# A transformer layer on 8 cores: the softmax-like normalisation moves to GpSimd, the masks to VectorE, the first layer norm's scaling to ScalarE

## The reference

```python
p = softplus(scores); p = p * p; p = p * causal
attn = p / (sum(p, -1) + 1e-9)
x = layernorm(x + (attn @ v) @ w_proj.T + b_proj)
h = gelu(x @ q8(W_fc).T + b_fc + 2 * (x @ A_fc.T) @ B_fc.T)          # f = 4096
x = layernorm(x + h @ q8(W_proj).T + b_proj + 2 * (h @ A_proj.T) @ B_proj.T)
```

## Time and profile before

| | us |
|---|---|
| median of 3 runs | 2142.27 (2140.19 to 2320.73) |
| the profiled execution | 2140.47 |
| span of its slowest core, core 3 | 2138.9 |
| spans of its cores | 2126.6 to 2138.9 |
| PE busy | 1929.6 (90%), 8834 matmuls |
| DVE busy | 1042.4 (49%) |
| ACT busy | 855.0 (40%) |
| POOL busy | 448.2 (21%) |

### The profile page before, as it was taken

How to read it: one execution, slowest core, us unless ns; L and a number is a source line. 1 busy time by engine, 2 the same in 40 slices (tenths; PEclk the granted TensorE clock), 3 DMA queues, 4 the chain that set the end, 5 groups by cost and what they waited for, 6 DMA issues and landing times.

```text
span 2138.9 us, 26841 instructions; the slowest of 8 cores (2126.6 to 2138.9 us)
## 1 busy us (share of the span) xinstructions
PE 1929.6 (90%) x8834; PEld 759.0 (35%) x8834; DVE 1042.4 (49%) x1613; ACT 855.0 (40%) x1026; POOL 448.2 (21%) x515
## 2 busy tenths in 40 slices
PE   6897987888987899999867889999999999999998
PEld 2332332222322333322222234444444444444443
DVE  2675887766689777788759731111110101020202
ACT  2464765765422466677533421212222121313130
POOL 1121221221156412222225421111010101010201
PEclk9998998999999999999978999999999999999999
DMA  8656554357466443344485465020202111110101
GB/s 130 149 135 146 155 150 131 100 128 149 122 188 181 131 112 116 114 124 128 125 222 163 133 191 169 30 69 30 70 30 59 40 50 50 50 60 20 60 10 49
DMA packets 118023, 228.35 MB, mean 107 GB/s; under 512 B 59282, under 2 KB 59538, under 8 KB 115186
## 3 DMA queue, kind: packets, MB, share of 16 engines
q1 hardware_dynamic: 109042, 195.03, 30.2%
q0 software_dynamic: 8848, 31.63, 8.7%
HBM read 182.21 MB, written 58.98 MB: 113 GB/s over the span
## 4 chain that ended last, share of the span: by engine, by line
PE 72%; DVE 10%; DMA 8%; issue 6%; POOL 2%; ACT 2%; SPq 0%; DVEq 0%; POOLq 0%; ACTq 0%
PE ps_s L924 20%; PE ps_a L976 10%; PE ps_f L976 10%; PE ps_a L718 8%; PE ps_f L341 8%; PE ps_s L674 6%; PE ps_f L365 5%; DVE a_ph L700 3%; DMA a_bc<-recscr 3%; PE ps_f L616 3%; DVE a_QO L776 2%; DMA recscr<-g_rec 2%; PE ps_f L497 2%; DMA g_den<-a_nd 1%; ACT a_ph L685 1%
## 5 line engine op out<-in xcount | busy, mean ns | idle before, releaser
L685 ACT ACTIVATE a_ph<-ps_s 128x1024 bf16<-128x1024 f32 (+1 forms) x576 | 560.7, 976 | 506.8 <-PE ps_s L674 505.4
L931 ACT ACTIVATE b_h<-ps_s,g_bfc,g_scl 128x512 bf16<-128x512 f32 x256 | 199.1, 778 | 649.1 <-PE ps_s L924 649.1
L924 PE MATMUL ps_s<-b_xT,b_Wfc 128*128 128x512 bf16 x2048 | 444.0, 379 | 0.0
L718 PE MATMUL ps_a<-a_ph,a_V 128*65 128x512 bf16 (+3 forms) x1280 | 354.0, 366 | 94.4 <-DVE a_ph L700 73.5
L700 DVE TENSOR_TENSOR a_ph<-a_ph 128x1024 bf16<-128x1024 bf16 (+1 forms) x576 | 399.9, 719 | 24.9 <-ACT a_ph L685 12.8
L341 PE MATMUL ps_f<-a_xT,a_wqk 128*128 128x512 bf16 x1024 | 307.5, 396 | 35.5 <-DMA a_xT<-xT 16.9
L692 POOL TENSOR_TENSOR a_ph<-a_ph,g_mask 128x256 bf16<-128x256 bf16 x256 | 196.4, 785 | 498.6 <-ACT a_ph L685 497.7
L981 DVE SCALAR_TENSOR_TENSOR g_x<-ps_a,g_scl,g_x 128x512 f32<-128x512 f32 x32 | 24.0, 751 | 566.1 <-PE ps_a L976 566.1
L924 PEld LDWEIGHTS ps_s<-b_xT,b_Wfc 128*128 128x128 bf16 x2048 | 200.4, 98 | 241.6 <-issue 0.2
L674 PE MATMUL ps_s<-a_QO,a_K 64*128 64x512 bf16 (+3 forms) x1280 | 226.3, 367 | 2.6 <-ACT a_QO L351 2.5
L976 PE MATMUL ps_a<-b_Wp,b_h 128*128 128x512 bf16 x1024 | 224.4, 379 | 0.0
(11 more groups left out here) (47 smaller groups left out, 937.1 us busy)
## 6 DMA issues: line engine op xcount, KB each, us to landing
a_w<-wfc SPq DMA_DIRECT2D x64, 512.0 KB, 5.7
a_w<-wpF SPq DMA_DIRECT2D x64, 512.0 KB, 4.5
a_bc<-recscr SPq DMA_DIRECT2D x64, 256.0 KB, 4.4
g_x<-x SPq DMA_DIRECT2D x32, 512.0 KB, 4.0
x1scr<-g_x SPq DMA_DIRECT2D x32, 512.0 KB, 4.0
g_x<-x1scr SPq DMA_DIRECT2D x32, 512.0 KB, 3.2
out<-g_x SPq DMA_DIRECT2D x32, 512.0 KB, 2.6
a_wqk<-wqk POOLq DMA_DIRECT2D x16, 512.0 KB, 7.4
```

Of the source, the lines that this page charges most:

```text
L685: s_read[sl] = P.op("scalar", lambda E: E.activation(dst, src, AF.Softplus, scale=HS ** -0.5), waits=[tok, ph_av[q]])
L718: tok = P.op("tensor", lambda E, c0=c0, n=n, off=off, x0=x0, hd=hd, fin=fin: E.matmul(ps_a[0:65, hd * 512 + c0: hd * 512 + c0 + n], V4[:, ...
L924: tok = P.op("tensor", lambda E, cc=cc, c0=c0: E.matmul(ps, b_Wfc[:, c0:c0 + 128], b_xT[:, (g % 2) * 4096 + cc * 512:(g % 2) * 4096 + (cc ...
L931: h_tok[(g, f)] = P.op("scalar", lambda E: E.activation(b_h[:, f * 512:(f + 1) * 512], ps, AF.Gelu, bias=g_bfc[:, f:f + 1], scale=g_scl[:, ...
```

## The change

1. **Normalisation on POOL.** Adding 1e-9 and the inverse (now a power -1, against a tile `g_m1` of -1) and both multiplications are POOL instructions. `pool_op` makes each of POOL's compute instructions wait for the one before it.
2. **Second head in the upper partitions.** The second head's A*V matmul takes 128 weight columns of `a_V`, shifted by one element: row 63 of the result is its denominator and rows 64 to 127 are its values. Its copy is 128x512, `a_bc` holds one head in the lower and one in the upper 64 partitions, and has two buffers, so turns are gone. Fetch and broadcast are two DMAs each instead of one. The relay's ticks are 1, 3, 5, 7 and 9.
3. **Masks on DVE**, behind the square and no longer ahead of it.
4. **First layer norm's scaling on ACT** (second layer norm: DVE as before), with one more small POOL instruction for the bias -mean*scale; it is emitted at the end of a projection chain and not in its middle. The load of x two tiles ahead moves from the chain's start to its middle.
5. **Merges behind the scores.** `merge_some` is called once in a tick, right behind `emit_scores`, and emits a merge if the chain in progress has 1 to 6 matmuls behind it. Merges are spread over windows 5 to 7 and 9 to 13 (before: also 14).
6. **Loads.** The first load of weights and x is split into halves and reordered; the absolute maxima use six slots (three of `a_w`, three of `g_x`).

The diff's core:

```diff
+        def pool_op(fn, waits):
+            pool_last[0] = P.op("gpsimd", fn, waits=list(waits) + [pool_last[0]])
+            return pool_last[0]
...
+        def load_first():
...
+            part(0)
+            rows(0)
+            rows(1)
+            part(1)
...
-                    yield 1.0 + merge_some(cc)
+                    yield 1.0
...
+            return k % 6 if k < 64 else k % 3
...
-        def merge_some(cc):
-
-            if cc not in (3, 6):
-                return 0.0
-            mg["seen"] += 1
-            if mg["want"] and mg["took"] * mg["of"] < mg["seen"] * mg["want"]:
+        def merge_some(part):
+
+            if not chains or mg["took"] >= mg["want"] * part:
+                return
+            c = chains[0]
+            if c.key[0] in ("qk", "v") and 1 <= c.done <= 6:
                 mg["took"] += 1
                 merge_half(mg["done"])
                 mg["done"] += 1
...
+            if n < NT:
+                ta = P.op("scalar", lambda E: E.activation(
+                    x, x, AF.Identity, bias=g_mv[:, q * 4 + 2:q * 4 + 3],
+                    scale=g_mv[:, q * 4 + 3:q * 4 + 4]), waits=[ln_wait.pop(n)])
...
+        def emit_square(u):
...
+            t = P.op("vector", lambda E: E.tensor_tensor(
+                ph[:, :, 0:n], ph[:, :, 0:n], ph[:, :, 0:n], ALU.mult), waits=[sp_tok[u]])
             if i < 3:
...
-                    mk_tok[u] = P.op("gpsimd", lambda E, off=off: E.tensor_tensor(
+                    t = P.op("vector", lambda E, off=off: E.tensor_tensor(
                         ph[:, :, off:off + 128], ph[:, :, off:off + 128], mk, ALU.mult),
-                        waits=[s_read[sl], k_mask])
+                        waits=[t, k_mask])
...
+                    if hd == 0:
+                        lhs, rows = a_V[:, x0:x0 + 65], 65
+                    else:
+                        lhs, rows = a_V[:, x0 + 1:x0 + 129], 128
...
             def recip():
+                den, rec = g_den8[:, b * 8:(b + 1) * 8], g_rec8[:, b * 8:(b + 1) * 8]
+                t = pool_op(lambda E: E.tensor_scalar(den, den, 1e-9, None, ALU.add),
+                         waits=[st[0], st[1]])
+                st["r"] = pool_op(lambda E: E.tensor_tensor(rec, den, g_m1[:, :], ALU.pow),
+                               waits=[t, k_m1])
...
             def spread_out():
+                for hd in range(2):
+                    st[2 + hd] = P.dma("sync", msem(f"bc{hd}{b}"), lambda E, hd=hd: E.dma_start(
+                        out=a_bc[hd * 64:hd * 64 + 64, b * 512:(b + 1) * 512],
+                        in_=d_rec[b:b + 1, hd * 512:(hd + 1) * 512].broadcast_to([64, 512])),
+                        waits=[st["d3"], bc_free[b]])
 
             def scale():
                 for hd in range(2):
+                    p0 = hd * 64
+                    t = pool_op(lambda E, hd=hd, p0=p0: E.tensor_tensor(
+                        a_QO[p0:p0 + 64, qslot(gp) + j * 512: qslot(gp) + (j + 1) * 512],
+                        a_nd[p0:p0 + 64, b * 1024 + hd * 512: b * 1024 + (hd + 1) * 512],
+                        a_bc[p0:p0 + 64, b * 512:(b + 1) * 512], ALU.mult),
+                        waits=[st[2 + hd], sc_pe[gp]])
...
             after_ticks(1, fetch)
-            after_ticks(4, recip)
+            after_ticks(3, recip)
             after_ticks(5, put)
-            after_ticks(7, turn)
+            after_ticks(7, spread_out)
+            after_ticks(9, scale)
...
-            mg["want"] = {5: 10, 6: 10, 7: 24, 9: 14, 10: 14, 11: 14, 12: 14, 13: 14, 14: 14}.get(gp, 0)
+            mg["want"] = {5: 11, 6: 11, 7: 24, 9: 16, 10: 16, 11: 16, 12: 17, 13: 17}.get(gp, 0)
...
                 emit_scores(u)
+                merge_some(1.0 - (cols_left - u_cols(u)) / cols_all)
```

More of the change, by code:

```diff
@@ L284, in __init__ @@
                 self.key, self.left, self.gen, self.after = key, cost, gen, after
+                self.done = 0
         def pump(budget):
@@ L296, in pump @@
                     c.left -= 1
+                    c.done += 1
                     budget -= step
@@ L339, in gen @@
                 for cc in range(CC):
-                    w = [k_wqk[gp], k_xT[(s, tg)], free] if cc == 0 else ()
+                    w = [k_wqk[(gp, which)], k_xT[(s, tg, 0)], free] if cc == 0 else [k_xT[(s, tg, cc // 4)]]
                     tok = P.op("tensor", lambda E, cc=cc: E.matmul(
@@ L725, in emit_av @@
                 if last:
-                    nd = a_nd[0:65, (ngrp[0] % 2) * 1024 + hd * 512:(ngrp[0] % 2) * 1024 + (hd + 1) * 512]
+                    nd = a_nd[0:rows, (ngrp[0] % 2) * 1024 + hd * 512:(ngrp[0] % 2) * 1024 + (hd + 1) * 512]
                     assert not nd_busy[ngrp[0] % 2]
@@ L840, in window @@
                 base = weave(main, extra)
-            mg["of"] = 2 * sum(c.key[0] in ("qk", "v") for c in base)
             return weave(base, spread)
@@ L895, in build_program @@
                         chains.append(c)
-                    cols_left = sum(u_cols(x) for x in range(NU) if wins[x] == gp)
+                    cols_all = cols_left = sum(u_cols(x) for x in range(NU) if wins[x] == gp)
                     carry = 0.0
                 emit_scores(u)
+                merge_some(1.0 - (cols_left - u_cols(u)) / cols_all)
             if 2 <= u <= NU + 1:
@@ L902, in build_program @@
             if u < NU:
-                left = sum(c.left for c in chains) + mg["want"] - mg["took"]
+                left = sum(c.left for c in chains)
                 carry = pump(carry + left * u_cols(u) / cols_left)
```

164 lines of the change are left out of this document (85 added, 79 removed).

## The result

| | before | changed |
|---|---|---|
| median, us | 2145.33 (2140.19 to 2320.73, 4 runs) | 2194.43 (2181.19 to 2372.02, 4 runs) |
| span of the slowest core | 2138.9 | 2179.7 |
| DVE busy | 1042.4 | 987.9 |
| POOL busy | 448.2 | 569.2 |

The changed kernel is 2.2% **slower**: ratio 1.0216, 95% interval 1.0123 to 1.031. So it is slower, and whether by more than 2% stays open. The forecast was 2030 us, 5.2% faster (range 1990 to 2105).

What follows compares the result with a forecast made beforehand. Before 1259 us, PE loses 200 us standing still and 76 us to slow clock, mostly awaiting DVE's squares behind late DMAs. Stretch gains sum to -119, +10 for squares held up by POOL: 2140.5 - 109 = 2031, said 2030 us (range 1990 to 2105).

Steps and rivals of the forecast that it cites:

- Second head in the upper partitions: Attention relay and A*V: larger copy and weight load cost nothing; 128 more SP DMAs, 60 us on a mostly waiting queue.
- slower rival: Normalisation relay gets too long, 28 us against 23 available, so copies stand waiting; 2220 us, chance 0.07.
- two other bounds: Upper bounds in the slower case's relay sum: POOL's power at 4.9 us and a multiplication at 2.4 us.
- The 160: Slower case: copies on ACT and DVE stand 5 us over, 32 times, 160 us in all.
- the relay at 16 us: Normalisation relay summed from start, fetch, inverse, write, broadcast and two multiplications: near 16 us, against 23 us for 14 ticks.
- Merges behind the scores ... I give it 5 us.: Attention part: one merge per tick with the scores already on their way, its eviction given more time; 5 us gained.
- ACT pays ... nothing, unless POOL's small instructions come late: Projection stretch: scaling adds 33 us to ACT, busy 41 of 135 us, at no cost unless POOL delays the Softplus.
- Nothing in the change touches that part: From 1259 us on PE is full at full clock, 870.5 of 880 us, so no change there.
- stage about 110: Projections, 600 to 735 us: DVE 79, PE 101, ACT 57, POOL 90; stretch falls to about 110, -25 us.
- the 25 I had put on its stage: Projection stretch, 600 to 735 us: expected gain of 25 us as scaling, masks and multiplications change engines.
- The squares held up by POOL: DVE's 576 squares each about 0.1 us slower from POOL's multiplications, some 60 us; 10 us counted against the gain.
- first rival, half the gain: Late DMAs move into POOL, which binds the projections, and its multiplications block DVE: 2085 us, chance 0.20.

Runs made afterwards that it cites:

- f1: Changed kernel with each head's denominators fetched to 64 partitions x 8 (32-byte pieces) and one contiguous write; ratio 1.0026 to the kernel before.
- f2: Changed kernel with f1's 32-byte pieces and the merge emitted behind the square in DVE's queue; ratio 0.9912 to the kernel before.
- g3: g1 with the first FFN tile's bias addition emitted in the FFN part, no longer in the last projection; ratio 0.9835 to the kernel before, the best version.
- b2: Kernel before with only the denominators' fetch split in two and fetch and write cut into 16-byte pieces; ratio 1.0245.
- g1: f2 with x's load and the layer norm's scaling (still on ACT) at their old places in the chain; ratio 0.9902 to the kernel before.
- h3: g3 with the first layer norm's scaling on DVE instead of ACT; ratio 0.9956 to the kernel before.
- g5: f2 with addition, inverse and multiplications back on DVE; ratio 1.0067 to the kernel before.
- b3: Kernel before with the denominators in 64 partitions x 16, pieces of 64 bytes; ratio 1.0018.

## Why the prediction was wrong

By stretch, change of length against the kernel before in us (window starts taken from the traces, one profiled execution each, slowest core):

| windows | forecast | changed | f1 | f2 | g3 | b2 |
|---|---|---|---|---|---|---|
| 0 | -6 | -3.8 | -2.5 | -2.4 | -3.7 | -3.6 |
| 1 to 6 | -48 | -6.3 | -20.2 | -31.0 | -35.8 | +13.3 |
| 7 | -5 | +10.5 | -0.7 | +3.3 | +1.9 | -0.3 |
| 8 (projections) | -25 | +11.0 | +11.3 | +10.5 | +2.8 | +1.7 |
| 9 to 13 | -3 | +35.6 | +32.3 | +11.3 | +14.8 | +31.7 |
| 14 | -32 | -17.9 | -22.6 | -21.9 | -17.0 | +10.5 |
| FFN | 0 | +11.7 | +12.1 | +9.7 | +1.7 | 0 |
| sum | -119 (+10) | +40.8 | +9.7 | -20.5 | -35.3 | +53.3 |

On the median of each run's eight cores the sums are the same within 3 us, and g3's column within 2, but not every stretch: window 8 is +7.1 changed, +4.9 in f1, +4.2 in f2 and +2.0 in g3, window 14 is -8.2 changed, and b2 loses 24 us in windows 1 to 6 and 13 in windows 9 to 13.

**The step that failed** is in "Second head in the upper partitions": "SP gets 2 more DMAs per group, 128 in all at some 0.5 us each, 60 us over 1259 on a queue that mostly waits", costed at nothing. The issue costs nothing that shows: f1 keeps both DMAs. What I left out was in the diff: `f=4` instead of `f=8`, pieces of 16 bytes instead of 32. That alone costs 41 us in the changed kernel and 52 us in the kernel before. I counted DMAs and not what they are cut into. My slower rival had "the doubled small DMAs at twice their time", but its sum doubled fetch and broadcast and left the write at 2 us, and the write is what took twice its time. I had also tied it to two other bounds that had no ground, and gave it 7%. Its mechanism, copies standing for the multiplication two groups earlier, came at 70 us of waits instead of 160. The 160 was miscounted: only one group in four is followed by 14 ticks (3 + 11 units), the others by 18 or 22, so it could strike 16 times and not 32. In the trace it struck three such groups, and the last window. I had put the relay at 16 us from landing medians alone. In groups 5 to 24 it took 17.9 before and 23.6 changed, where 14 ticks are 25 us (387.5 us for 216 ticks; my 23 was of windows 9 to 13), so on the mean next to nothing was left, and the three groups that held up a copy took 25.6 to 40.5.

**Second, "Merges behind the scores ... I give it 5 us."** I asked whether the merge's own wait is shorter (it is longer, 133 us instead of 92), and not what stands behind it on DVE. The square does, and the place costs some 24 us (f1 to f2), most of it in windows 9 to 13, which I had put at -3.

**Third, "ACT pays ... nothing, unless POOL's small instructions come late".** They did, 57.2 us in 16 waits, and at one place, the border of the FFN part, PE stood behind it. The other waits cost nothing that shows: g3 has 89.2 us of them in 28 waits and is the fastest. "Nothing in the change touches that part" was wrong by 11.7 us, of which g3 gives 10 back.

**Fourth, the sizes of stages.** g3 has all three mended, which gives back 82 us (1.0216 to 0.9835); it is at -35, not -109, so the other half of the miss lies here. The largest gap is window 8: "stage about 110" came from adding up POOL's busy time; it took 146.8 changed and 138.6 in g3, with POOL 88 of 138 us busy and DVE 87. No engine is full, so a chain of waits sets its length. The critical path over window 8, in the kernel before and in the changed one, names it:

```profile
by line: issue 24.2%; DVE a_ph L700 11.2%; PE ps_f L341 9.6%; DVE g_x L622 8.0%; DVE g_st L569 5.6%; DVE g_x L586 5.3%; DVE g_st L571 4.9%; PE ps_f L616 4.6%; POOL g_mv L577 4.0%; POOL g_mv L574 3.7%; POOL g_x L559 3.5%; PE ps_a L718 3.2%; 
by line: DMA g_x<-x 21.3%; DMA x1bscr<-g_x 17.2%; PE ps_f L367 11.1%; issue 9.6%; POOL g_x L602 9.2%; PE ps_f L668 4.6%; DMA x1scr<-g_x 3.8%; POOL a_QO L834 3.8%; PE ps_a L776 3.6%; DVE a_ph L745 2.8%; DVE g_x L674 2.4%; DVE a_ph L750 2.3%; 
```

Before, the path runs over DVE's instructions, and the window takes 135.8 us on every core. Changed, it runs over transfers: the stores of a finished tile of x and the load of the next tile into the slot that they free, 52 to 62 us of the path on each core, none before. My sum had no term for them. In g1 and g3, with the order of before, they are still 19 to 37 us of it (45 to 64 in f2), and the window takes 137 to 138 us on the median core. Without ACT's scaling it would be 16 us longer (h3). What else keeps it from 110 is open. In windows 9 to 13 g3 keeps +14.8 us, 12.4 of them PE standing still; the 12 merges more are there too, and their share is not separated. Window 14 falls short by 15 us: the last projections still wait for the last multiplication (24.0 us in g3, 19.4 before).

Three readings of the forecast were wrong as well, and change little. POOL is 14 to 22% busy outside the projections, not 20 to 38; the 38 is of a stretch that has projections. PE stands still for a larger share of the first and fourth stretches (25 and 22%, clock 0.97 and 0.96) than of the second (16%, 0.91), so the low clock doesn't keep to where it stands most. And the 0.867 us of a square in the projections is a mean of both widths, whose mean over the run is 0.719 and not 0.756.

**What held.** Multiplication 1.27 us (median; forecast 1.2), power 1.68 (1.5), copy of 128 rows 0.69 (65 rows: 0.68), weight load of 128 columns no dearer. The scaling on ACT took 1.24 us instead of 1.02, and the mask 0.40 on the mean instead of 0.27, 102 us on DVE instead of 69:

```profile
L834 POOL TENSOR_TENSOR a_QO<-a_nd,a_bc x128: 1252/1269/1892, 62.9 to 1273.5; 64x512 bf16<-64x512 f32 x128
L815 POOL TENSOR_TENSOR g_rec<-g_den,g_m x64: 1667/1677/2577, 46.7 to 1264.3; 128x8 f32<-128x8 f32 x64
L750 DVE TENSOR_TENSOR a_ph<-a_ph,g_mask x256: 291/293/2266, 27.9 to 1234.0; 128x256 bf16<-128x256 bf16 x128
L776 PEld LDWEIGHTS ps_a<-a_ph,a_V 128*65 128x65 bf16 x640 | 71.7, 116 | 223.2 <-issue 180.3
L776 PEld LDWEIGHTS ps_a<-a_ph,a_V 128*128 128x128 bf16 x640 | 62.8, 102 | 59.6 <-issue 19.8
```

(The first three rows are least, median and longest in ns.) The two moves that carried the forecast pay, once the rest is mended: the normalisation on POOL 33 us (g5), the scaling on ACT 26 us (h3). That the latter is near the 25 I had put on its stage is luck: 16 of the 26 stand in window 8, and that stage is no shorter than before. The squares held up by POOL were over-counted for most of the run: in windows 1 to 6 those of 1024 columns rose from 723 to 745 ns on the mean, not by 100; in window 8, both widths together, they rose from 867 to 991. g3 is nearest to my first rival, half the gain, and only one of its reasons is seen: copies still wait 41 us for POOL's multiplication, in 4 waits at two groups, while the squares are slowed by a fifth of what it took, and POOL doesn't bind the projections.

## What to carry to other kernels

Read a moved DMA by its innermost contiguous piece on both sides, not by its count or bytes: here a cut from 32 to 16 bytes cost 41 and 52 us, at least about as much as either of two good moves brought (33 and 26). Before moving an instruction that waits for another engine within an in-order queue, name what stands right behind it; if that is what the critical engine waits for, it belongs one place later. And when a relay's spare time matters, measure the relay in the trace rather than sum its transfers' medians. When instructions leave a busy engine, ask what the critical path will run over next, transfers and the slots that they free included, and read a stage's length on all cores: g1's slowest shows no change in window 8 where most of the others do.

## What the hardware did unexpectedly

- 4 KB written to memory landed after 1.7 us in 128 pieces of 32 bytes (before), 1.9 in 64 of 64 bytes (b3), and 3.7 in 256 of 16 bytes (b2), and large transfers beside it landed later in b2 (5.8 instead of 4.5 us for 512 KB). The single packet of 16 bytes is no slower than that of 32, 9 ns.
- The power -1 costs 1.68 us for 128x8, against 0.61 for the power -0.5 of 128x1: neither by column nor fixed, if the exponent makes no difference, which no run shows.
- The mask on DVE takes 0.40 us on the mean, and once 2.27. POOL's two-input instructions hold it up, as the scaling in the earlier trace rows: the 194 masks that overlap none of them take 0.29 us on the mean and at most 0.32, the 62 that overlap one take 0.73.
